# Summing gathered rows in a graph network kernel: products signalled and added in twos in the first gather layer and in threes in the second, with twelve one-hots

## What is computed

```python
x = x + _L0_gnn_ref(_layernorm(x), src, dst, ...)   # gather by src, sum by dst, mean, batch norm, relu
x = x + _L0_ffn_ref(_layernorm(x)[None], ...)[0]    # 8 experts, one for each token
x = x + _L1_gnn_ref(_layernorm(x), edge_index, ...) # gather by dst, weighted sum by src, three products
x = x + _L1_ffn_ref(_layernorm(x)[None], ...)[0]    # 8 experts, two for each token

# the gather of the first graph layer
msgs = feat_src[src]
sums = jax.ops.segment_sum(msgs, dst, num_segments=n)
# and of the second
msgs = xw[col_sl] * norm[:, None]
h7 = jax.ops.segment_sum(msgs, row_sl, num_segments=N) + b
```

## Time and profile before

| | us |
|---|---|
| median of 3 runs | 3348.91 |
| lowest and highest run | 3347.49, 3348.94 |
| the profiled execution | 3348.88 |
| its span, first to last instruction | 3347.1 |
| first layer's gathers, first to last start | 83.5 to 1134.1 |
| second layer's gathers, first to last start | 1804.2 to 2846.4 |

### The profile page before, as it was taken

The page is one execution under the profiler, slowest core; times in us unless marked ns, Lnnn a source line. Parts: engine busy times, 40 slices in busy tenths (PEclk is TensorE's granted clock), DMA queues, the critical chain, the costliest instruction groups (busy, mean ns, idle before and its releaser), DMA issues. The chain is left out here.

```text
span 3347.1 us, 50072 instructions
## 1 busy us (share of the span) xinstructions
PE 2756.0 (82%) x13577; PEld 2042.1 (61%) x13577; DVE 2383.6 (71%) x6179; ACT 1317.9 (39%) x3355; POOL 2175.5 (65%) x2178
## 2 busy tenths in 40 slices
PE   7777777988998879987997777777777776799999
PEld 6444444777777645556885455555555554599998
DVE  6887999999999776656776666666666666554443
ACT  7445676777877544440111011111111111245554
POOL 2777777777777544204665777777777777166666
PEclk9999989999999889998998788888887778799999
DMA  6333333333333445435565444444444445333444
GB/s 208 104 105 104 103 105 107 110 110 111 110 109 111 121 121 153 151 119 158 184 207 153 118 136 136 137 137 136 136 136 136 136 137 118 68 60 64 69 67 58
DMA packets 209866, 405.73 MB, mean 121 GB/s; under 512 B 48293, under 2 KB 131838, under 8 KB 209328
## 3 DMA queue, kind: packets, MB, share of 16 engines
q0 software_dynamic: 124624, 303.07, 35.2%
q1 hardware_dynamic: 83136, 97.49, 8.8%
q10 hardware_dynamic: 1824, 1.84, 0.2%
HBM read 316.98 MB, written 88.96 MB: 121 GB/s over the span
## 5 line engine op out<-in xcount | busy, mean ns | idle before, releaser
L819 PE MATMUL bank<-ring_or_weights,normed 128*128 128x257 f32 (+1 forms) x3320 | 1141.0, 451 | 471.4 <-issue 265.2
L819 PEld LDWEIGHTS bank<-ring_or_weights,normed 128*128 128x128 f32 x3320 | 610.8, 214 | 870.1 <-issue 520.4
L776 DVE TENSOR_TENSOR acc_or_weights<-bank,acc_or_weights 128x257 f32 (+1 forms) x1660 | 700.6, 422 | 407.7 <-PE bank L819 370.4
L833 POOL DMA_INDIRECT ring_or_weights<-gather_table,item_other_node x830 | 799.0, 963 | 255.3 <-issue 221.8
L833 POOL DMA_INDIRECT ring_or_weights<-scaled_and_whole_rows,item_other_node x830 | 790.7, 953 | 255.2 <-issue 226.6
L764 DVE TENSOR_SCALAR normed<-iota_row,item_local_node,item_weight 128x128 f32<-128x128 f32 x830 | 298.0, 360 | 7.4 <-issue 7.4
L1139 ACT ACTIVATE acc_or_weights<-iota_row,ring_or_weights 128x128 f32<-128x128 f32 x782 | 284.9, 391 | 7.0
L2368 POOL DMA_INDIRECT out_rows<-normed x112 | 177.9, 1589 | 124.8 <-DVE normed L2243 101.7
L1063 ACT ACTIVATE normed<-normed,edge_records_by_src 128x64 f32<-128x64 f32 x784 | 207.9, 339 | 62.4 <-DVE normed L1038 61.2
L2326 PE MATMUL bank<-normed 128*128 128x128 f32 x1792 | 221.6, 278 | 0.0
L1077 PEld LDWEIGHTS bank<-normed 128*128 128x128 f32 x1564 | 207.0, 193 | 13.1
(11 more groups left out here) (365 smaller groups left out, 4241.4 us busy)
## 6 DMA issues: line engine op xcount, KB each, us to landing
hidden_rows<-normed SPq DMA_DIRECT2D x49, 512.0 KB, 2.7
ring_or_weights<-gather_table,item_other_node POOLq DMA_INDIRECT x830, 2.8
ring_or_weights<-scaled_and_whole_rows,item_other_node POOLq DMA_INDIRECT x830, 2.8
acc_or_weights<-in_L_ffn_Wd SPq DMA_DIRECT2D x8, 1024.0 KB, 5.6
acc_or_weights<-in_L_ffn_W SPq DMA_DIRECT2D x16, 512.0 KB, 7.3
hidden_rows<-x_rows SPq DMA_DIRECT2D x7, 896.0 KB
gather_table<-normed SPq DMA_DIRECT2D x24, 258.0 KB, 3.6
normed<-scaled_and_whole_rows SPq DMA_DIRECT2D x24, 256.0 KB, 4.7
```

The lines of the kernel that those rows point to most:

```text
L776: v.tensor_tensor(into, sum_bank(l, i)[:, 0:width], into, ALU.add).then_inc(added, 1)
L819: m.matmul(sum_bank(l, i)[:, 0:width], lhsT=hot, rhs=ring[:, i % RING, 0:width], start=True, stop=True).then_inc(sum_made, 1)
L833: g.indirect_dma_start(ring[:, i % RING, 0:D], None, table, IndirectOffsetOnAxis(ap=gidx[:, i:i + 1], axis=0)).then_inc(ring_in[i % RING], 16)
```

## The change

`TOGETHER` = (2, 3) is new. Items are taken in groups of two in the first layer and of three in the second.

- **Signal.** Only the last product of a group adds one to `sum_made`. `made_with(l, items)` turns a number of items into the number of signals that covers them, rounded up, and stands wherever `sum_made` is waited for: in `one_hots`, `one_hot`, `add_sums` and in POOL's wait.
- **Banks.** Only the first product of a group waits on `added`, for the banks of the whole group.
- **Adds.** `added_by(l, i, lag)` says which adds stand at item `i` on DVE: none, or those of a whole group one behind the other. Each add keeps both of its waits.
- **One-hots of the second layer.** The ring has 12 in place of 8, is filled 5 ahead in place of 4, and starts 2048 bytes lower; since rows that POOL stores lie there until then, DVE waits for these stores (`wait_scattered_rows`) before the first one-hot.
- **Heads.** They stand two items later (`HEAD_LAG` = 4 in place of `SECOND_LAG` = 2 in `when_on_time`).

```diff
-    HOT_RING, HOT_LEAD, SECOND_LAG = 8, 4, 2
+    HOT_RING, HOT_LEAD, SECOND_LAG, HEAD_LAG = 12, 5, 2, 4
+    TOGETHER = (2, 3)
-    onehot = space(36864, HOT_RING * P).rearrange("p (n c) -> p n c", c=P)
+    onehot = space(34816, HOT_RING * P).rearrange("p (n c) -> p n c", c=P)
+    def made_with(l, items):
+        return l * -(-ITEMS // TOGETHER[0]) + -(-items // TOGETHER[l])
+
     def one_hots(b):
-            v.wait_ge(sum_made, (b - 1) * HOTS)
+            v.wait_ge(sum_made, made_with(0, (b - 1) * HOTS))
     def one_hot(i):
-            v.wait_ge(sum_made, ITEMS + i - HOT_RING + 1)
+            v.wait_ge(sum_made, made_with(1, i - HOT_RING + 1))
     def add_sums(l, i, width, regs):
-        v.wait_ge(sum_made, l * ITEMS + i + 1)
+        v.wait_ge(sum_made, made_with(l, i + 1))
+    def added_by(l, i, lag):
+        n = TOGETHER[l]
+        return max(0, (i - lag) // n * n), max(0, (i + 1 - lag) // n * n)
+
     def aggregate_vector(l, width, beside):
         if l:
+            wait_scattered_rows(v)
...
             beside(i)
-            if i >= lag:
-                add_sums(l, i - lag, width, regs)
-        for i in range(ITEMS - lag, ITEMS):
+            for j in range(*added_by(l, i, lag)):
+                add_sums(l, j, width, regs)
+        for i in range(added_by(l, ITEMS, lag)[0], ITEMS):
             add_sums(l, i, width, regs)
     def aggregate_tensor(l, width, beside):
+            last = min(ITEMS, i // TOGETHER[l] * TOGETHER[l] + TOGETHER[l])
-            if i >= nbank:
-                m.wait_ge(added, l * ITEMS + i - nbank + 1)
-            m.matmul(sum_bank(l, i)[:, 0:width], lhsT=hot,
-                     rhs=ring[:, i % RING, 0:width], start=True, stop=True).then_inc(sum_made, 1)
+            if i >= nbank and i % TOGETHER[l] == 0:
+                m.wait_ge(added, l * ITEMS + last - nbank)
+            product = m.matmul(sum_bank(l, i)[:, 0:width], lhsT=hot,
+                               rhs=ring[:, i % RING, 0:width], start=True, stop=True)
+            if i + 1 == last:
+                product.then_inc(sum_made, 1)
     def aggregate_gpsimd(l, table, beside):
             if i >= RING and i % 4 == 0:
-                g.wait_ge(sum_made, l * ITEMS + min(ITEMS, i + 4) - RING)
+                g.wait_ge(sum_made, made_with(l, min(ITEMS, i + 4) - RING))
     def when_on_time(gi, n):
-        return HALVES * min(T, G2 * (gi + 1)) // 2 + MARGIN + SECOND_LAG + step
+        return HALVES * min(T, G2 * (gi + 1)) // 2 + MARGIN + HEAD_LAG + step
```

More of the change, by code:

```diff
@@ L2010, in heads @@
                 if i:
-                    v.wait_ge(added, ITEMS + min(i - SECOND_LAG, ITEMS))
+                    v.wait_ge(added, ITEMS + (added_by(1, i, SECOND_LAG)[0] if i < ITEMS else ITEMS))
                 v.wait_ge(pair_in[gi % 3], 32 * (gi // 3 + 1))
```

## The result

The changed kernel takes 3407.34 us (median of 4 runs, 3406.87 to 3408.18) against 3348.2 before: the ratio is 1.0181, with a 95% interval of 1.0168 to 1.0193. It is 59 us slower; 3395 was forecast, with a range of 3358 to 3415.

The account below looks back on a forecast made before the run. POOL's gathers were taken as the bound in both layers, DVE close behind in the first. 3348.9 us + 44 (first layer) + 1 (second layer) + 1 (later heads) = 3395 us, range 3358 to 3415.

Parts of the forecast that it names:

- The bound: Both layers: POOL's gathers set the pace; in the first layer DVE is a near second with some 2% to spare.
- The price of a pair: First layer, DVE: 0.28 us for each add newly behind another, 0.61 us to the next start against 0.33.
- The rival without a price: Rival: the second add's wait is swallowed or semaphores cost nothing; time stays at 3349 us; chance 0.08.
- Items 350 to 799: First layer: 179 new places cost 50.1 us; DVE needs 609.6 against POOL's 571, so 34.6 us are lost.
- Items up to 349: First layer: 7.7 to 14 us added in items 200 to 299, of which 9 us reach POOL.
- has room: Items 150 to 199 and 300 to 349: some 6 and 7 us of add waits, but DVE just catches up less.
- the ring: First layer: DVE may fall about 8 us behind before POOL stops; 4 us of backlog hidden in items 300 to 349.
- a whole pair ahead: First layer: with four banks PE can be two products ahead, so DVE, once behind, finds its products ready.
- The second layer: Groups of three: 154 us of add waits covered by 313 us of product waits; +1, and +1 for later heads.
- Part of it hidden: Rival: the ring gives 8 us at both tight places and more DVE waits were free; 3372 us, chance 0.12.
- faster: Rival: blocks of adds disturb POOL's gathers less, up to 20 us come back; 3329 us, chance 0.05.
- Slower still: Rival: no wait swallowed (64 us) and rounded-up signals stop POOL at many heads (15 us); 3428 us, chance 0.07.

Follow-up runs that it names:

- runs with a buffer apart: Changed kernel, from item 366 each pair's second add to its own buffer: without wait on the first 3372.04 us beside 3349.26; twin keeping it 3808.04 beside 3745.61.
- run without the wait: Changed kernel, but from item 366 of the first layer each pair's second add uses its own buffer, not waiting for the first: 3372.04 us beside 3349.26.
- adds only: Changed kernel, but first layer's products each signal and wait for their own bank, adds still paired: 3399.2 us beside 3347.07; slow chip 3736.71 beside 3710.22.
- signals only: Changed kernel, but first layer's adds one at each item, signal and bank wait still for two: 3364.21 us beside 3347.07; slow chip 3806.82 beside 3710.22.

## Why the prediction was right, and where it was off

- **The bound.** Right: POOL without a wait in front of the gathers, DVE 2% behind it. DVE had 0.02 us an item to spare, the pairs took 0.11, and the bound changed over.
- **The price of a pair.** 0.28 us was taken from two rows, and the row of the second add named PE's product as what ended its wait, not the add before it; that the price is the add's was shown only by the runs with a buffer apart. The changed kernel shows 0.62 against 0.34. The waits of add for add came to 81.2 us in 403 times in the first layer, where some 85 were forecast. The rival without a price is out. The Trainium skill ("VectorE: DVE Perf Modes", "The DRAIN you can't avoid") says that a semaphore after each operation costs nothing extra. This case's traces don't agree for two adds of which the second waits for the first: the wait takes 0.19 us.
- **Items 350 to 799.** DVE's need was put 38.6 us above POOL's 571, and 34.6 of them were to be lost. The adds fall 39.8 us further behind there, and the gathers lose 34.3. The run without the wait takes this part away.
- **Items up to 349, the step that was off.** I let 9 us reach POOL; it was 23.6, and that is the whole difference between 44 and 58. Three things were wrong in it. First, the pairs of items 150 to 199 and 300 to 349 were called free because DVE "has room" there. They weren't: the adds are 7.0 us late at item 199, so DVE enters the tight stretch with that much of the ring gone, and they lose another 4.4 us in items 300 to 349. Second, of the 14.0 us of items 200 to 299 I let 9 through, since waits would swallow some. Hardly any did: the adds lose 14.2 us there in adds only and 15.5 in the changed kernel. Nearly all of the lateness reached the gathers, since the add of item 299 was 13 us behind its gather already before (475.1 against 462.1 us). Third, the coarser signal and bank wait were costed at nothing on PE ("a whole pair ahead"); with paired adds they cost 7 us on top (58.1 against 51.3 at the last gather), and DVE is 4 us of them later at item 199 already. What the ring gives was right: 4 us were to be hidden behind item 349, and 5.5 were.
- **The second layer.** +2 was forecast; the gathers took 0.5 us less, and what follows them ended 58.7 us later where the last gather was 58.0 later, so under 1 us for the heads. In the other runs with this second layer its gathers took 1042 to 1047 us. The rounded-up signal stopped POOL nowhere there: 0.3 us remains the longest wait for a product in that layer.
- **The other rivals.** "Part of it hidden" and "faster" are out: gathers are as long as before at the median, and POOL's busy time in the first layer fell by only 3 us (799.0 to 796.2). "Slower still" named the right direction for the first layer, as hardly a wait of DVE was swallowed up to item 349, but it put 64 us there, not 58, and stops of POOL in the second layer that never came. The sum was 12 us short because of one part, the smaller of the first layer's two; the rest came out as it was put down.

## What to carry to other kernels

Ask on which engine a signal or a wait is saved: here they were saved on PE, which did not set the pace, and paid for on DVE, the engine next to the bound. Before putting dependent instructions in a row, look at what stands between them now: other work between two adds to the same place hides the wait of the second for nothing. And room in front of a tight stretch is not free time: DVE used it to come to item 200 on time, and when it came 7 us late there was nothing left to hide what followed.

## What the runs showed of the hardware

- From the start of one 128x257 add to the next that waits for it, 0.62 us with a register in the address and 0.52 without (and one column less); 0.33 if it doesn't wait for it. The add's own record is 0.42 us long, so a follower that doesn't wait starts before it ends.
- The same kernel took 3348, 3710 and 3746 us on different chips; in the traces from the slow two, signals of products came 2.1 to 5.3 us late in the place shown, and an add waited up to 9.7 us. The order of two variants turned round there: adds only beat signals only by 70 us, and lost to it by 35 us elsewhere. A comparison of schedules holds for the chip's condition in which it was made.
